# Attention with its value sums in 512-column matmuls, a mask matmul for the first tile, and four small jobs moved between the vector engines

## The reference, cut to what matters

```
cq  = rms_norm(x @ w_qa.T, q_a_ln_w)                    # 192 query latents
ckv = x @ w_kva.T                                       # 64 key/value latents and 64 rotary key columns
k_pe = k_pe * cos + rotate_half(k_pe) * sin
scores = einsum('bhqd,bhkd->bhqk', q_full, k_full) * scale
scores = where(causal, -inf, scores)
attn = softmax(scores)
out = einsum('bhqk,bhkd->bhqd', attn, v)                # 16 heads
return out.transpose(0, 2, 1, 3).reshape(b, s, H * DV) @ w_o.T
```

## Time and profile before

| | |
|---|---|
| median of 3 runs | 2003.1 us (1998.96 to 2003.15) |
| profiled execution, its own time | 2002.72 us |
| its span, first to last instruction | 2000.9 us |
| mean granted TensorE clock | 0.973 of full speed |
| busy share: PE, DVE, ACT, POOL | 93%, 74%, 52%, 42% |
| attention, first scores to last sums | 1007 to 1761 us |
| one sequence of it, in the steady part | 48.0 us |

### The profile page before, as it was taken

One profiled execution on the slowest core, in us unless ns is written; L12 is line 12 of the kernel. 1 busy time (PEld: TensorE's weight loads), 2 busy tenths in 40 slices (PEclk: granted clock), 3 DMA queues, 4 the chain that ended last, 5 costly groups with the idle time before them and its releaser, 6 DMA issues. The chain is left out here.

```text
span 2000.9 us, 35701 instructions
## 1 busy us (share of the span) xinstructions
PE 1852.4 (93%) x12032; PEld 1659.3 (83%) x12032; DVE 1483.2 (74%) x4168; ACT 1038.9 (52%) x2694; POOL 833.2 (42%) x865
## 2 busy tenths in 40 slices
PE   7999999999999979999799999999999999977980
PEld 6788888888888868888589999999999999977880
DVE  8978778787778756666477888888888888863436
ACT  5534333333334324333277777777777777734653
POOL 1232323232332320000144466666666666754775
PEclk9999999999999989999899999999999999998995
DMA  3201000010100114474100010000000000126868
GB/s 127 85 1 33 12 22 22 11 32 1 32 1 22 34 55 136 148 258 138 38 12 17 18 41 28 21 21 20 19 19 20 19 19 14 39 73 172 204 140 255
DMA packets 102004, 118.82 MB, mean 59 GB/s; under 512 B 12567, under 2 KB 93723, under 8 KB 101184
## 3 DMA queue, kind: packets, MB, share of 16 engines
q1 hardware_dynamic: 89104, 108.42, 17.1%
q0 software_dynamic: 12288, 8.11, 2.7%
q10 hardware_dynamic: 432, 0.02, 0.0%
HBM read 75.50 MB, written 57.10 MB: 66 GB/s over the span
## 5 line engine op out<-in xcount | busy, mean ns | idle before, releaser
L239 POOL TENSOR_TENSOR rwkv_gate<-rwkv_key,rwkv_gate 128x512 f32<-128x512 f32 x128 | 204.1, 1595 | 524.5 <-DVE rwkv_key L444 524.5
L1451 POOL TENSOR_TENSOR kept_raw<-kept_raw,mla_row_inv 128x512 f32<-128x512 f32 x192 | 199.3, 1038 | 265.5 <-DVE mla_row_inv L1802 264.6
L312 ACT ACTIVATE rwkv_gate<-rwkv_r 128x512 f32<-128x512 f32 x128 | 76.6, 598 | 400.7 <-DVE rwkv_o_low L365 398.1
L1610 ACT ACTIVATE kept_raw<-kept_raw,mla_least 128x256 f32<-128x256 f32 (+1 forms) x512 | 227.7, 446 | 78.9 <-DVE mla_least L1786 77.2
L1786 DVE CUSTOM_DVE_ANT_0 kept_raw<-mla_score,kept_mask 128x256 f32<-128x256 f32 (+1 forms) x512 | 156.8, 352 | 82.9 <-PE mla_score L2159 53.0
L429 DVE TENSOR_TENSOR rwkv_kv<-rwkv_v,rwkv_key 128x512 f32<-128x512 f32 x128 | 88.1, 688 | 124.4 <-PE rwkv_v L477 122.2
L436 DVE TENSOR_TENSOR_SCAN rwkv_state<-rwkv_decay_w,rwkv_kv 128x256 f32<-128x256 f32 x256 | 166.2, 692 | 4.1
L494 PE MATMUL rwkv_out<-rwkv_w_high,rwkv_o_high 128*128 128x256 f32 x512 | 144.2, 282 | 5.3 <-DVE rwkv_o_low L365 5.3
L494 PE MATMUL rwkv_out<-rwkv_w_high,rwkv_o_low 128*128 128x256 f32 x512 | 145.5, 284 | 0.0
L494 PE MATMUL rwkv_out<-rwkv_w_low,rwkv_o_high 128*128 128x256 f32 x512 | 144.4, 282 | 0.0
L1536 POOL DMA_INDIRECT slots<-mla_x_out,mla_slot_now x128 | 129.4, 1011 | 31.1 <-issue 24.5
(11 more groups left out here) (397 smaller groups left out, 6085.8 us busy)
## 6 DMA issues: line engine op xcount, KB each, us to landing
kept_raw<-in_experts SPq DMA_DIRECT2D x27, 384.0 KB
kept_raw<-in_rkvo SPq DMA_DIRECT2D x16, 512.0 KB
moe_y_in<-sums SPq DMA_DIRECT2D x32, 256.0 KB, 4.9
sums<-ffn_empty SPq DMA_DIRECT2D x12, 512.0 KB
slots<-ffn_empty SPq DMA_DIRECT2D x16, 361.2 KB
moe_e_rows<-slots SPq DMA_DIRECT2D x32, 180.6 KB
kept_x_in<-x SPq DMA_DIRECT2D x18, 256.0 KB
mla_x_res<-x SPq DMA_DIRECT2D x17, 256.0 KB
```

The costliest lines, as they stand in the source:

```text
L239: nc.gpsimd.tensor_tensor(gate[:, c % 2, :], key[:, c % 2, :], gate[:, c % 2, :], ALU.mult).then_inc(gated_done, 1)
L1451: nc.gpsimd.tensor_tensor(unit, unit, row_inv[:, v % PR, 0:len(heads)].rearrange("p (h a) -> p h a", a=1) .to_broadcast([P, len(heads), ke ...
L1610: last = nc.scalar.activation(probs[:, v % PR, i * keys:(i + 1) * keys], masked[:, v % 2, i * keys:(i + 1) * keys], ACT.Exp, bias=least[:, ...
```

## The change

- The values of a key block become one stationary operand, 64 columns of high parts beside 64 of low parts (`v_parts`), and the moving operand is all 512 columns of four heads. High and low probabilities make two matmuls for each key block. The result holds the sum over high values in partitions 0 to 63 and that over low values in 64 to 127.
- ACT copies the lower half out of PSUM (`keep_low_sums`), DVE adds the upper half to it in two instructions that also bring the heads into their places (`add_sums`), a slot later ACT makes the high part (`sums_high`) and POOL the low part (`sums_low`).
- For the first tile, PE adds the mask by a bf16 matmul of the identity with the mask repeated four times; DVE only reduces the bank to the row extremes; ACT takes the exponentials straight from PSUM, and PE waits for those before it reuses that bank.
- ACT copies the latents out of PSUM (`lat_rows`) ahead of the squares; DVE scales from there; the rotary key moves from DVE to POOL (`rotate_key`), behind each `latent_rstd`.
- Two router steps with an immediate (L1905, L1919) take a tile in its place; `q_turn` and `values_low` need an instruction less; four memsets at the start go.

```diff
 weighted_sums:
-                    pe.wait_ge(o_low, group - 1)
-                terms = [(b, kb, vp, pp) for kb in range(keys // P) for b in range(2) for vp, pp in PARTS]
+                    pe.wait_ge(o_added, group - 1)
+                terms = [(kb, pp) for kb in range(keys // P) for pp in range(2)]
...
-                    last = nc.tensor.matmul(out, v_part[vp][:, seq % 2, kb, b, :], probs_t, start=(i == 0),
+                    last = nc.tensor.matmul(bank[:, :], v_parts[:, seq % 2, kb, :], probs_t, start=(i == 0),
 scores:
-                wait_reuse(pe, masked_done, m, 2)
+                if m >= 2:
+                    pe.wait_ge(exp_done if heads_of((m - 2) % SLOTS)[0] == 0 else masked_done, m - 1)
+                if tile == 0:
...
+                    nc.tensor.matmul(score_ps[v % 2][:, :], ident_first[:, :], mask_first[:, :, :], start=True, stop=False)
 mask_scores (DVE):
+                if tile == 0:
+                    nc.vector.tensor_reduce(least[:, v % 2, :], score_ps[v % 2][:, :].rearrange("p (h k) -> p h k", h=HG),
+                                            axis=AX.X, op=ALU.min).then_inc(masked_done, 1)
+                    return
 ACT:
+                nc.scalar.activation(lat_rows[:, n % 2, :], ps[:, 0:LATC], ACT.Copy)
+            def keep_low_sums(seq, v):
...
+                nc.scalar.activation(low_sum[:, group % 2, :], bank[KVL:, :], ACT.Copy).then_inc(low_kept, 1)
 DVE:
+            def add_sums(seq, v):
...
+                for b in range(2):
+                    last = nc.vector.tensor_tensor(o_whole[b * KVL:(b + 1) * KVL, group % 2, :, :], high[:, :, b, :],
+                                                   low[:, :, b, :], ALU.add)
+                last.then_inc(o_added, 1)
 POOL:
+            def rotate_key(n):
+                pool.wait_ge(squared, n + 1)
+                t, at = n % 2, QLR + KVL
+                raw = lat_rows[:, t, at:at + DR]
+                nc.gpsimd.tensor_tensor(k_turn[:, t, 0, :], raw, rk[:, 0, t, :], ALU.mult)
+                nc.gpsimd.tensor_tensor(k_turn[:, t, 1, :].rearrange("p (a d) -> p a d", a=2),
+                                        raw.rearrange("p (a d) -> p a d", a=2)[:, ::-1, :],
+                                        rk[:, 1, t, :].rearrange("p (a d) -> p a d", a=2), ALU.mult)\
+                    .then_inc(k_turned, 1)
+                pool.wait_ge(k_turned, n + 1)
+                nc.gpsimd.tensor_tensor(k_rows[:, t, KVL:], k_turn[:, t, 0, :], k_turn[:, t, 1, :], ALU.add)\
+                    .then_inc(k_roped, 1)
+            def sums_low(seq, v):
+                group, _, where = sums_of(seq, v)
+                pool.wait_ge(o_high, group + 1)
+                nc.gpsimd.tensor_tensor(o_part[1][where], o_whole[:, group % 2, :, :], o_part[0][where].bitcast(F32),
+                                        ALU.subtract).then_inc(o_low, 1)
 POOL, slot:
                 if kind == "latent" and v == 9:
                     latent_rstd(n)
+                    rotate_key(n)
+                m, of, vs = slot_before(seq, v, SUM_LAG + 2)
+                if m >= 0 and completes(vs):
+                    sums_low(of, vs)
                 m, of, v1 = slot_before(seq, v, 1)
                 if m >= 0:
                     scale_probs(m, v1)
...
                 if v == 10 and exists(seq + 2):
                     latent_rstd(2 * (seq + 2) + 1)
+                    rotate_key(2 * (seq + 2) + 1)
```

More of the change, by code:

```diff
@@ L1244, in attention_phase @@
         p_scaled = s.sem("p_scaled")
+        low_kept = s.sem("low_kept")
+        o_added = s.sem("o_added")
         o_high = s.sem("o_high_done")
@@ L1594, in values_high @@
                 act.wait_ge(lat_done, 2 * seq + 2)
-                act.wait_ge(v_zeroed, 1)
                 if seq >= 2:
                     act.wait_ge(summed, 8 * (seq - 1))
[L1598 to L1601, removed]
+                nc.scalar.activation(v_parts[:, par, :, 0:KVL], k_rows[:, :, 0:KVL], ACT.Copy).then_inc(v_high, 1)
             def exps(seq, v):
@@ L1614, in exps @@
                 last.then_inc(exp_done, 1)
+            def keep_low_sums(seq, v):
+                group, bank, _ = sums_of(seq, v)
+                act.wait_ge(summed, group + 1)
+                if group >= 2:
+                    act.wait_ge(o_added, group - 1)
+                nc.scalar.activation(low_sum[:, group % 2, :], bank[KVL:, :], ACT.Copy).then_inc(low_kept, 1)
             def sums_high(seq, v):
-                group, src, where = sums_of(seq, v)
-                act.wait_ge(summed, group + 1)
-                nc.scalar.activation(o_part[0][where], src, ACT.Copy).then_inc(o_high, 1)
+                group, _, where = sums_of(seq, v)
+                act.wait_ge(o_added, group + 1)
+                nc.scalar.activation(o_part[0][where], o_whole[:, group % 2, :, :], ACT.Copy).then_inc(o_high, 1)
             def probs_high(m, v):
@@ L1646, in slot @@
             def slot(seq, par, v):
+                m, of, vs = slot_before(seq, v, SUM_LAG + 2)
+                if m >= 0 and completes(vs):
+                    sums_high(of, vs)
                 for t in late_turns(seq, v):
@@ L1734, in split_turn, with latent @@
                                             ALU.subtract).then_inc(turn_read, 1)
-            def latent(n, t, ps=proj_ps):
+            def latent(n, t):
                 dve.wait_ge(lat_rstd_done, n + 1)
[L1739 to L1754, removed]
@@ L1757, in values_low @@
                 dve.wait_ge(v_high, seq + 1)
[L1758 to L1762, removed]
+                nc.vector.tensor_tensor(v_parts[:, par, :, KVL:], k_rows[:, :, 0:KVL],
+                                        v_parts[:, par, :, 0:KVL].bitcast(F32), ALU.subtract).then_inc(v_low, 1)
@@ L1771, in q_turn @@
                                         rq[:, 0, tile:tile + 1, :].to_broadcast([P, 8, DR]), ALU.mult)
[L1772 to L1777, removed]
+                nc.vector.tensor_tensor(
+                    q_sin[:, c, :].rearrange("p (h a d) -> p h a d", a=2, d=DR // 2), q[:, :, ::-1, :],
+                    rq[:, 1, tile:tile + 1, :].rearrange("p o (a d) -> p o a d", a=2)
+                    .to_broadcast([P, 8, 2, DR // 2]), ALU.mult).then_inc(q_turned, 1)
             def mask_scores(seq, v):
@@ L2173, in weighted_sums @@
                 tile, _, keys = heads_of(v)
-                group, out, _ = sums_of(seq, v)
+                group, bank, _ = sums_of(seq, v)
                 wait_turned(pe, "p", v, seq)
```

93 lines of the change are left out of this document (60 added, 33 removed).

## The result

The changed kernel takes 2045.4 us (median of 4 runs, 2043.1 to 2047.2) against 2002.5 (4 runs, 1999.0 to 2003.2): a ratio of 1.0218, 95% interval 1.0205 to 1.0231. The forecast was 2009, with 1988 to 2027 as its range: the sign and the ring were right, the size was not. The profiled execution spans 2044.1 us, 43.2 more than before.

A forecast was written before the change was run, and what follows sets the result against it. PE bounds the kernel before; after the change POOL's ring would, 1.0 us more a sequence. Sequences 3 to 13 give 11.0, 14 +0.5, 0 and 1 -3.8, 2 -1.1, 15 0: +6.6 on 2002.7, so 2009 us, range 1988 to 2027.

The forecast's parts named there:

- the ring: PE's slot 0 to POOL's start, POOL's work, back to PE: sets the pace at 49.0 us a sequence; chance 0.55.
- its two prices: Time of new instructions on POOL: 0.69 us for a low part, 0.98 us for a rotary key.
- PE's four new waits: Forecast had three, some 3 us a sequence: first tile's low parts (slot 10), router's membership (slot 11), `probs_low` (slot 0).
- Those 5.4 us meet 4.2 of play: On POOL, five low parts and two keys, 5.4 us, against 3.75 us of holes plus 0.45 of slack.
- the run: POOL from slot 2's probabilities, taken up in slot 3, to its third router step: 31.0 us, forecast 32.7.
- Its first leg stays near 15.5 ... I take 15.3: From PE's slot 0 to POOL's start on slot 2's probabilities: 15.5 us before, 15.3 forecast.
- The sum on DVE: DVE's added and removed work nearly cancels: busy 40.4 us a sequence stays about 40, under PE's.
- ACT's new wait: ACT waits for `o_added` at the head of a slot; any loss, some tenths, is covered by 8 us idle.
- the last leg: From the end of POOL's third router step back to PE: 1.5 us, less 0.45 of slack.
- the wait for `o_added`: Sign of being wrong: PE waiting for `o_added`, which the prediction held covered by more than a microsecond.
- Waits pile up: Rival: DVE, ACT and POOL hand values on in four steps instead of two; 2021 to 2027 us; chance 0.18.
- PE stays the bound: Rival: POOL's new work falls into its holes, PE gains 1.9 us a sequence; 1973 us; chance 0.24 for all.

The follow-up runs named there:

- x1: Kernel before the change, with two more scratch subtractions of 128x256 on POOL in slot 6: 2005.5 us, ratio 1.0018.
- x2: Kernel before the change, with two more scratch subtractions of 128x256 on POOL in slot 10, straight ahead of the router steps: 2019.3 us, ratio 1.0090.
- e2: Changed kernel, with ACT writing the router's exponentials (the odds) into PSUM instead of SBUF: 2032.4 us, ratio 1.0153 to the kernel before.
- e3: Changed kernel, with the low part of the sums subtracted by DVE instead of POOL: 2054.6 us, ratio 1.0274 to the kernel before.
- e1: Changed kernel, with both rotary keys moved on POOL behind the third router step of slot 10: 2030.5 us, ratio 1.0148 to the kernel before.
- x3: Changed kernel, with ACT's high part of the sums behind the splits at the head of a slot: 2033.0 us, ratio 1.0156 to the kernel before.
- p1: Changed kernel with mask and latents undone, leaving the 512-column sums with their hand-over and POOL's low part: 2032.5 us, ratio 1.0159 to the kernel before.
- c1: Changed kernel with the edits of e1 and e2, and four of eight scatters issued in slots 1 and 2: 2016.7 us, ratio 1.0079 to the kernel before.
- c2: c1 with ACT's order of x3, tail scatters in their old place, DVE's seventh router step behind slot 6's additions: 1996.6 us, 0.9971 to the kernel before.

## Why the prediction was wrong

*The ring and its two prices* held. The key at 0.98 (measured 0.99 and 1.00) and the low part at 0.69 (0.70 to the next start) are not where the 43 us come from, and three of PE's four new waits are where they were foreseen.

*"Those 5.4 us meet 4.2 of play"* is the step that failed first. It summed three holes and the slack behind them, as if work anywhere in the run could use all of it. x1 and x2 show that work uses only what lies behind it. Ahead of slot 7's scaling the new work fell into holes; behind it stood 1.09 + 0.45 us of play and came two keys and two low parts, 2.0 + 1.4 = 3.4 us. That is 1.9 us a sequence, where 1.2 (5.4 less 4.2) was put.

*"Its first leg stays near 15.5 ... I take 15.3"* failed by 0.9 us. It is the odds instruction, which is held while POOL makes the low part that the change puts into slot 3; e2 takes the leg back to 15.3, and e3, without that low part, to 15.2. The forecast counted instructions of DVE by their own durations and none for what POOL does meanwhile. L1948, the router's sum, was put at 0.17 with its immediate gone, and lasts 0.87 beside POOL's scaling, more than the 0.63 of before; e1, where it takes 0.15, shows that some 0.5 us of the first leg hang on it. The sum on DVE, "near nothing", came out as 2.9 us.

*ACT's new wait*, "which its 8 us of idle time cover", does not cost ACT but DVE, which waits 0.97 us in slot 8 for the split behind it. In the changed kernel POOL's run hides that (x3 takes the wait away, and the run is no shorter); in p1 and c1 the wait is there too, and c2, which takes it away together with one in slot 6, gains 0.65 us.

Together: 30.05 us from slot 0 to slot 7's scaling became 30.87, the 16.45 from there to the membership became 18.83, and the last leg gave back 0.45: 2.75 us a sequence instead of 1.0, 30 us instead of 11.

*The clock* was not in the sum: 5.8 us in the changed kernel, some 11 in e1. That waits of PE precede it fits, but a stretch as idle (7.41 of 10.24 us busy, 1438.98 to 1449.22) is not followed by it; what decides was not found.

*The ends.* Sequences 0 to 2 were to give 4.9 us, and 1.0 is gained up to their end: in sequence 1 PE's busy time falls by 1.4 us (44.75 to 43.39), not 1.9, and half of that goes into new waits. Sequence 15 was put at 0 because POOL had holes there; PE waits 2.9 us for the additions and 1.8 for POOL. The first of these is the wait for `o_added` that the prediction held covered by more than a microsecond and named as a sign of being wrong. In the tail the last group is handed from engine to engine with nothing else for PE to do:

```profile
1806.17 0.38 PE L2185 MATMUL mla_turn<-kept_wvo_high,mla_o_high 128*128 128x256 f32 x1 [3.53 <-POOL mla_o_low L1478]
```

That is 0.59 + 0.85 + 0.42 + 0.73 for its four steps and 0.8 of waiting for POOL, which issues a scatter, where two steps stood before. These two were read from the traces, not tried.

*The rivals.* "Waits pile up" was the nearest, but it rested on stretched instructions of POOL; those kept their prices, and it was DVE's that stretched. "PE stays the bound" is what c2 shows in part: with the run and DVE freed, 0.55 us a sequence of the gain arrives.

## What to carry to other kernels

Idle time on an engine covers new work only if it lies behind that work, between it and whatever waits for its end: for each hole, ask which work stands after it. Before work is moved to GpSimd, list what VectorE does on SBUF at that moment: here each held the other up. A value that is handed through more engines also makes each of them wait at the head of its list, so look at what stands behind those waits: exchanging two steps there brought 12 us (x3), more than the 5 us by which the best form of the change beats the kernel before (c2).

## What the runs showed of the hardware that was not expected

A DVE instruction of 0.20 us, begun 0.35 us ahead of POOL's low part and while POOL was issuing a scatter, is recorded until 0.07 us after the low part's end (1413.49 against 1412.68 + 0.74 = 1413.42). Beside the scatter alone it takes 0.20 us before the change and 0.32 in e3. Replacing an immediate by a tile, both operands in SBUF, does not free an instruction either: L1948, of 128x2 values, takes 0.87 us beside POOL's scaling, and 0.16 in the two last sequences, where POOL is idle at that moment.
